# Normalised attention and displacement layer, one core: key/value matmuls moved between the products with V, the second layer spread over the next batch, denominators split over two engines

## The reference

```python
x = x + attention(group_norm(x))        # 32 groups over 24 channels each
x = x + displace(group_norm(x))
# attention, 12 heads of 64 channels: k and v from the last two thirds of W_qkv (q is not used);
#   var_k and var_v = their variances over a head's channels, one number per position
#   scores = var_v @ var_k.T / 8;  softmax;  attn @ v;  @ W_proj.T + b_proj
# displace: 48 bands of 16 channels, each shifted by its own whole offset (zeros come in), then a 3x3 depthwise filter
#   that is a product of a column filter and a row filter
```

## Time and profile before

| | us |
|---|---|
| median of 3 runs | 2329.48 (2328.37 to 2331.11) |
| profiled execution, its own time | 2330.09 |
| its span, first to last instruction | 2328.3 |
| PE busy | 2002.9 (86%) |
| VectorE busy | 1949.5 (84%) |
| ScalarE busy | 1102.4 (47%) |
| POOL busy | 296.2 (13%) |
| mean granted clock of PE, of 2.4 GHz | 0.931 |

### The profile page before, as it was taken

One profiled execution on the slowest core, in us unless ns is written; L12 is line 12 of the kernel. 1 busy time (PEld: TensorE's weight loads), 2 busy tenths in 40 slices (PEclk: granted clock), 3 DMA queues, 4 the chain that ended last, 5 costly groups with the idle time before them and its releaser, 6 DMA issues.

```text
span 2328.3 us, 30324 instructions
## 1 busy us (share of the span) xinstructions
PE 2002.9 (86%) x8804; PEld 788.2 (34%) x8804; DVE 1949.5 (84%) x3547; ACT 1102.4 (47%) x1139; POOL 296.2 (13%) x172
## 2 busy tenths in 40 slices
PE   3998898888988899898997989888898889988850
PEld 2432343323432234322442234332343224432220
DVE  7479959898698986899788996989869898699938
ACT  5249411792237911396115941179223791149601
POOL 2000023000320012100230002300032001210003
PEclk8999999899999999998998999989999999999985
DMA  4222214222242212423044221422224221242104
GB/s 177 113 110 66 90 39 145 92 83 73 61 141 101 65 65 90 166 73 101 3 130 143 63 93 39 145 98 77 73 61 141 101 65 64 90 171 68 47 25 138
DMA packets 106453, 214.37 MB, mean 92 GB/s; under 512 B 53538, under 2 KB 54306, under 8 KB 106274
## 3 DMA queue, kind: packets, MB, share of 16 engines
q1 hardware_dynamic: 93954, 171.44, 23.1%
q10 hardware_dynamic: 12320, 40.77, 5.0%
HBM read 154.08 MB, written 57.74 MB: 91 GB/s over the span
## 4 chain that ended last, share of the span: by engine, by line
issue 61%; DVE 10%; PE 9%; SPq 8%; DMA 4%; POOL 4%; ACT 3%; ACTq 0%; DVEq 0%; POOLq 0%
DVE ox L732 4%; SPq L399 4%; PE ps L1030 4%; PE ps L970 4%; SPq L394 3%; POOL vx L457 3%; ACT ring L582 2%; DVE st L680 1%; DVE h_sp L794 1%; PE ps L1012 1%; DMA shift_rows<-ox 1%; DMA rb_x<-gs_rows_x 1%; DMA ox<-in_L_conv_W_qkv 1%; POOL ox L476 1%; SPq L406 1%
## 5 line engine op out<-in xcount | busy, mean ns | idle before, releaser
L970 PE MATMUL ps<-wkv_hi,h_sp 128*128 128x512 f16 x2304 | 717.2, 390 | 26.6 <-ACT vx L526 19.8
L582 ACT ACTIVATE ring<-a_sb,coef 128x1024 f32<-128x1024 f32 x624 | 660.3, 1134 | 139.0 <-DVE h_sp L794 80.6
L1012 PE MATMUL ps<-ring,vx 128*64 128x512 f32 x2496 | 600.0, 628 | 44.7 <-ACT ring L582 42.0
L794 DVE TENSOR_TENSOR h_sp<-h_sp,ring 128x1024 f32<-128x1024 f32 x464 | 543.2, 1227 | 0.0
L970 PE MATMUL ps<-wkv_lo,h_sp 128*128 128x512 f16 x1152 | 448.9, 390 | 0.0
L1030 PE MATMUL ps<-ox,wp_hi 128*128 128x512 f16 x1152 | 346.7, 382 | 0.0
L970 PEld LDWEIGHTS ps<-wkv_hi,h_sp 128*128 128x128 f16 x2304 | 230.3, 100 | 319.3 <-issue 30.1
L680 DVE BATCH_NORM_STATS2 st<-ps 128x6 f32<-128x64 f32 x1536 | 217.5, 216 | 135.5 <-PE ps L970 130.2
L1012 PEld LDWEIGHTS ps<-ring,vx 128*64 128x64 f32 x2496 | 182.1, 144 | 434.6 <-issue 318.3
L526 ACT ACTIVATE vx<-ps 128x256 f32<-128x256 f32 (+1 forms) x128 | 62.5, 489 | 419.9 <-DVE st L680 419.9
L732 DVE SCALAR_TENSOR_TENSOR ox<-ox,taps 128x992 f32<-128x992 f32 (+1 forms) x160 | 244.4, 1527 | 3.0
(11 more groups left out here) (124 smaller groups left out, 1528.0 us busy)
## 6 DMA issues: line engine op xcount, KB each, us to landing
a_sb<-a_rows SPq DMA_DIRECT2D x64, 512.0 KB, 5.9
ox<-in_x SPq DMA_DIRECT2D x48, 512.0 KB, 6.0
shift_rows<-ox SPq DMA_DIRECT2D x48, 512.0 KB, 3.2
out<-ox SPq DMA_DIRECT2D x48, 512.0 KB, 2.7
vx<-in_x ACTq DMA_DIRECT2D x42, 512.0 KB, 6.1
a_sb<-a_rows ACTq DMA_DIRECT2D x32, 512.0 KB, 6.8
h_sp<-r_rows SPq DMA_DIRECT2D x64, 256.0 KB, 3.9
ox<-shift_rows SPq DMA_DIRECT2D x240, 64.0 KB, 2.0
```

Source lines behind the costliest of these rows:

```text
L582: nc.scalar.activation(ring_t[i % RING], a_sb[:, h % 4, :], ACT.Exp, scale=coef[:, h, m:m + 1]).then_inc(s_exp, 1)
L794: nc.vector.tensor_tensor(acc[p % 2][s], one, ring_t[i % RING], ALU.add).then_inc(s_acc, 1)
L970: last = nc.tensor.matmul(ps[:, kv_bank[u % 4], :], h_sp[:, k, hp, m * P:(m + 1) * P], wkv[wpart][:, k, c * HALF:(c + 1) * HALF], start=(k ...
L1012: last = nc.tensor.matmul(ps[s * HD:(s + 1) * HD, o_bank[p % 3][j], :], v_sb[:, m, (2 * p + s) * HD:(2 * p + s + 1) * HD], ring_t[(i + s) ...
```

## The change

- Key and value columns are now ordered by pair of heads: 24 units again, but a unit is two position tiles of one pair, 2 x 18 matmuls of 256 columns in one bank, and only two banks are used in turn. The first eight units (pairs 0 and 1) stay in stage A. The other sixteen are issued by PE between the products with V: four in each of the pairs 0 to 3, after m = 0, 2, 4, 6. The loop now turns between stages B and C.
- var_v rows, key maxima and coefficients are made per pair: two transposes and one small matmul on PE, some small VectorE instructions, and a write and two broadcasts on SP's queue for each pair. They went once per batch (in two parts) before, and four of the broadcasts were on ACT's queue.
- The ring has eight tiles (four m), not ten.
- Denominators: VectorE adds only the tiles m below MD[p] = 7, 7, 7, 7, 5, 5. The other tiles go straight through the ones matmuls, which now have 32 output partitions and write all into one bank. ScalarE copies the result (d_copy) where VectorE did. The last pair goes the way of the others, through DRAM; its in-place reciprocal is gone.
- The second layer of batch b is spread over the pairs of batch b+1, one channel tile at a time, in one buffer for the shifted tile and one for the taps. Its group norm and its mask are one VectorE instruction (gn) where POOL had two (L469, L476); the mask is now applied before the shift. POOL keeps only the power of -1/2; the first layer's norm goes from POOL to ScalarE. In the last batch six buffers are used.
- x1 tiles are loaded one by one as they come free (x1_reload); the next batch's x is loaded by ACT in pair 4 and its statistics are taken in pair 5, where stage C had them. Two partly done units of the output projection are issued in pair 5.
- In the first batch SP writes the zero pads before the offsets.

The diff, cut to what the text speaks of (removed functions are those printed above; the indentation is cut by eight):

```diff
-RING = 10
-CH = KV // HALF
+PC = 4 * HD
+UQ = MT // 2
+NU = NP * UQ
+RING = 8
+NA_RING = 3
...
-kv_bank = (0, 1, 4, 5)
-pj_bank = (2, 3, 4, 5)
-o_bank = ((2, 3), (0, 1), (6, 7))
-d_bank = (4, 5)
+kv_bank = (0, 1)
+o_bank = (2, 4)
+pj_bank = (0, 1, 2, 3, 7, 6)
+D_BANK = 6
...
+MD = (7, 7, 7, 7, 5, 5)
+ADDS_TO = [0]
+for n in MD:
+    ADDS_TO.append(ADDS_TO[-1] + 2 * (n - 1))
+NADD = ADDS_TO[NP]
+def add_count(p, s, m):
+    return ADDS_TO[p] + 2 * (max(m, 1) - 1) + s + 1
+def acc_of(p, s):
+    return acc[:, (2 * p + s) % NA_RING, :]
+def ring_of(p, s, m):
+    return ring[:, ((p * MT + m) * 2 + s) % RING, :]
+def a_count(b, h):
+    return b * 48 + 16 * (h // 4 + 1)
...
+    def span(b, l1, with_next):
+        later = l1 is not None
+        a_write(b, 0)
+        a_broadcast(b, 0, later)
         for p in range(NP):
+            if p == 0:
+                a_write(b, 1)
+                if later:
+                    g_store(l1, 1)
+                a_broadcast(b, 1, later)
+                if later:
+                    g_windows(l1, 1)
+                    out_store(l1, 0)
+                    g_store(l1, 2)
+                    x1_reload(l1, 0)
+                    g_windows(l1, 2)
+                    out_store(l1, 1)
+                continue
+            d_rows(b, p - 1)
+            r_write(b, p - 1)
+            if p < NP - 1:
+                a_write(b, p + 1)
+            if later:
+                x1_reload(l1, p)
+            r_broadcast(b, p - 1, later)
+            if p < NP - 1:
+                a_broadcast(b, p + 1, later)
+                if later:
+                    if p + 2 < CT:
+                        g_store(l1, p + 2)
+                        g_windows(l1, p + 2)
+                    out_store(l1, p + 1)
+        if with_next:
+            stats_to_groups(sp, "x", b + 1)
+        d_rows(b, NP - 1)
+        r_write(b, NP - 1)
+        if with_next:
+            stats_out(sp, "x", b + 1)
+        r_broadcast(b, NP - 1, later)
+        if with_next:
+            stats_to_channels(sp, "x", b + 1)
...
+    def body(b, with_next):
+        y_chain(b)
+        g_store(b, 0)
+        g_windows(b, 0)
+        span(b + 1, b, with_next)
...
+    def v_evict(b, u):
+        q, g = divmod(u, UQ)
+        act.wait_ge(s_bn, b * NU + u + 1)
+        src = ps[:, kv_bank[u % 2], :].rearrange("p (m c) -> p m c", m=2)
+        nc.scalar.activation(v_sb[:, q, 2 * g:2 * g + 2, :], src[:, :, 0:P], ACT.Copy, scale=V_DOWN).then_inc(s_vev, 1)
+    def exps(b, p, m):
+        for s in (0, 1):
+            h = 2 * p + s
+            i = (p * MT + m) * 2 + s
+            if m == 0:
+                if s == 0:
+                    act.wait_ge(s_coef, b * NP + p + 1)
+                act.wait_ge(s_a[h % 4], a_count(b, h))
+            if i >= RING:
+                pj, mj = divmod((i - RING) // 2, MT)
+                act.wait_ge(s_pv, b * (NT // 2) + (i - RING) // 2 + 1)
+                if mj < MD[pj]:
+                    act.wait_ge(s_acc, b * NADD + add_count(pj, s, mj))
+            nc.scalar.activation(ring_of(p, s, m), a_sb[:, h % 4, :], ACT.Exp,
+                                 scale=coef[:, h, m:m + 1]).then_inc(s_exp, 1)
+    def d_copy(b, p, later):
+        act.wait_ge(s_d, b * NP + p + 1)
+        if later or p:
+            act.wait_ge(s_dt, (b * NP + p) * 64)
+        nc.scalar.activation(d_sb[:, :], ps[:, D_BANK, :], ACT.Copy).then_inc(s_dsb, 1)
...
+    def span(b, l1, with_next, beside=None):
+        later = l1 is not None
         for p in range(NP):
+            nxt = (p + 1) * UQ
             for m in range(MT):
+                if not later and p == 0 and m == 3:
+                    act.wait_ge(s_pads, 2 * CT * 16)
+                exps(b, p, m)
+                if m == 0 and 1 <= p <= 4:
+                    v_evict(b, nxt + 1)
+                if m == 1 and p == 0 and later:
+                    middle_tap(l1, 0)
+                if m == 2 and p <= 4:
+                    v_evict(b, nxt + 2)
+                if m == 3:
+                    if p:
+                        d_copy(b, p - 1, later)
+                    if p <= 4:
+                        v_evict(b, nxt + 3)
+                    if p == 4 and with_next:
+                        load_x(b + 1)
+                if m == 4 and 1 <= p <= 4 and later:
+                    middle_tap(l1, p + 1)
+                if m == 5 and p:
+                    add_bias(b, p - 1)
+                if m == 6 and p <= 3:
+                    v_evict(b, nxt + UQ)
...
+    def kv_stats(b, u):
+        q, g = divmod(u, UQ)
+        dve.wait_ge(s_kv, b * NU + u + 1)
+        for m in (0, 1):
+            for c in range(4):
+                lo = m * 2 * P + c * HD
+                ins = nc.vector.bn_stats(st[:, 2 * g + m, c, :], ps[:, kv_bank[u % 2], lo:lo + HD])
+        ins.then_inc(s_bn, 1)
...
+    def k_max(b, q, later):
+        dve.wait_ge(s_ktp, b * NP + q + 1)
+        if later or q:
+            dve.wait_ge(s_arow, (b * NP + q) * 16)
+        nc.vector.tensor_reduce(kmx1[:, :], ps_kt, AX_X, ALU.max).then_inc(s_kch, 1)
+        nc.vector.tensor_copy(at[:, :], ps_at).then_inc(s_at, 1)
+        dve.wait_ge(s_kch, b * NP + q + 1)
+        nc.vector.tensor_scalar(kdiag[:, :], ident[0:2, 0:2], kmx1[:, 0:1], None, ALU.mult).then_inc(s_kdiag, 1)
...
+    def add_up(b, p, m, later):
+        if not 1 <= m < MD[p]:
+            return
+        for s in (0, 1):
+            i = (p * MT + m) * 2 + s
+            if m == 1:
+                if s and (later or p):
+                    dve.wait_ge(s_d, b * NP + p)
+                one = ring_of(p, s, 0)
+            else:
+                dve.wait_ge(s_acc, b * NADD + add_count(p, s, m - 1))
+                one = acc_of(p, s)
+            dve.wait_ge(s_exp, b * NT + i + 1)
+            nc.vector.tensor_tensor(acc_of(p, s), one, ring_of(p, s, m), ALU.add).then_inc(s_acc, 1)
...
+    def gn(b, t, dst, wait_taps=True):
+        if t == 0:
+            dve.wait_ge(s_msk, b + 1)
+        elif wait_taps:
+            dve.wait_ge(s_pch, b * 4 * CT + 4 * (t - 1) + 2)
+        nc.vector.scalar_tensor_tensor(dst.rearrange("p (y x) -> p y x", x=W),
+                                       x1[:, t, :].rearrange("p (y x) -> p y x", x=W), rb["y"][:, t, 1:2],
+                                       mask_y[:, t:t + 1, :].broadcast_to((P, H, W)),
+                                       ALU.subtract, ALU.mult).then_inc(s_gn, 1)
...
+    def phase_a(b, l1, beside=None):
+        for u in range(2 * UQ - 1):
+            kv_stats(b, u)
+            if l1 is not None:
+                if u == 0:
+                    group_var(dve, "y", l1)
+                if u == 1:
+                    group_spread_y(dve, l1)
+            if u == UQ - 1:
+                variances(b, 0)
+                if l1 is not None:
+                    masks_y(l1)
+                    gn(l1, 0, g_t)
             if beside is not None:
                 beside(u)
...
+    def span(b, l1, with_next, beside=None):
+        later = l1 is not None
         for p in range(NP):
+            nxt = (p + 1) * UQ
+            if p >= 2:
+                o_second(b, p - 2)
+            if p <= 4:
+                kv_stats(b, nxt + 3)
+                variances(b, p + 1)
+            for m in range(MT):
+                add_up(b, p, m, later)
+                if m == 1 and p == 5 and with_next:
+                    x_stats(b + 1, (0, 1))
+                if m == 2:
+                    if p:
+                        d_reciprocal(b, p - 1)
+                    if p <= 4:
+                        k_max(b, p + 1, later)
+                    if p == 0 and later:
+                        taps_y(l1, 0, g_t, t_t)
+                        gn(l1, 1, g_t)
+                        taps_x(l1, 0, t_t)
+                    if p == 5 and with_next:
+                        x_stats(b + 1, (2, 3))
+                if m == 3:
+                    if p <= 3:
+                        kv_stats(b, nxt + UQ)
+                    if p == 5 and with_next:
+                        x_stats(b + 1, (4, 5))
+                        channel_aggregate("x", b + 1)
+                if m == 4:
+                    if p:
+                        o_normalise(b, p - 1)
+                    if p <= 4:
+                        k_scales(b, p + 1)
+                if m == 5:
+                    if p <= 3:
+                        kv_stats(b, nxt + UQ + 1)
+                    if 1 <= p <= 4 and later:
+                        taps_y(l1, p + 1, g_t, t_t)
+                        if p + 2 < CT:
+                            gn(l1, p + 2, g_t)
+                if m == 6:
+                    if p <= 3:
+                        kv_stats(b, nxt + UQ + 2)
+                    if p == 0 and later:
+                        taps_y(l1, 1, g_t, t_t)
+                        gn(l1, 2, g_t)
+                    if p <= 4 and later:
+                        taps_x(l1, p + 1, t_t)
+                if beside is not None:
```

(81 more changed lines are left out.)

858 lines of the change are left out of this document (367 added, 491 removed).

## The result

The changed kernel takes 2366.28 us (median of 4 runs, 2363.57 to 2372.53), the kernel before 2328.93 us beside it. The ratio is 1.0165, with a 95% interval of 1.014 to 1.0189: the change makes the kernel some 1.65% slower. The forecast was 2317 us, with "faster" the likeliest sign.

The account below looks back on a forecast made before the run. PE was taken to bound stages C, A and the middle pairs, VectorE the old stage B and pair 5. 279 + 7 x 274.3 + 113 = 2312 us span, 2313 as run time, plus 4 for handovers: 2317; range takes in 2265 to 2375.

Parts of the forecast that it names:

- four small DMAs 2.3 to issue ... and 1.8 to land: Stage C, chain of pair 5's output: denominator rows through DRAM; whole chain 14.8 us, hidden beside PE's 16.7.
- PE 13.7 + 4 sets 3.4 + 2.4 = 19.5: Pair 4: TensorE's products, four denominator sets and a further 2.4 give 19.5 us.
- The rival that came near: Middle pairs: the reciprocal's DMAs queue behind SyncE's windows; 36 us per pair, cycle +8.5, 2376 us; chance 0.25.
- the rows of landing were measured among such moves: Argument against the slower reciprocal-chain rival: measured landing times already included neighbouring 512 KB moves.
- Pair 5: Last pair of a batch: VectorE bounds it, ending 21 us after pair 4.
- The head: First batch, to its last denominator set: 279 us, before 269.7; SP free for a_write at 83.5.
- Stage A and pair 0: Batch start: first product at 44.5 us into stage A, then pair 0 takes 45 us, held by evictions and VectorE.
- PE idles 12 us: Stage A's end: a_write behind eight windows on SP delays the first product; called the change's largest loss.
- if a_sb lands sooner: Listed way to be wrong: the broadcast tiles land earlier in stage A because VectorE reaches gn(0) sooner.
- The unit prices: TensorE: 256-column matmul 0.11 us, unit of 36 matmuls 3.96, 32-partition denominator set 0.86, mode-change excursion 0.26.
- 0.76 us per excursion: Alternative price of a tiling-mode change on TensorE if a drain lasts 0.38 us: 12 us more per batch.
- Stage C: From the last denominator set: 43.8 us, before 46.9, including PE waiting 2.5 for pair 4's output split.

Follow-up runs that it names:

- e1: Changed kernel with load_x moving 4 columns per tile instead of 1024 (10 KB, not 3 MB per batch), same six DMAs: 2325.1 us.
- e4: Changed kernel with the first batch's six x1 loads issued behind the first row write and broadcasts instead of ahead: 2363.2 us.
- e8: Changed kernel with next-x loads behind pair 3's split, first-batch x1 behind the first row broadcasts, next batch's first rows ahead of the windows: 2283.4 us.
- e5: Changed kernel with the next batch's first a_write and a_broadcast ahead of the eight windows in SyncE's order: 2321.8 us.
- e2: Changed kernel with the next batch's x loads moved from step 3 to step 7 of pair 4, behind pair 3's split: 2339.5 us.
- e12: Changed kernel with the next batch's x loads behind add_bias in step 5 of pair 4: 2366.0 us.
- e7: Changed kernel with the denominator split undone: VectorE adds all eight steps of every pair, TensorE does one ones set per pair: 2515.2 us.
- e3: Changed kernel with VectorE doing k_max of the next pair ahead of the previous pair's reciprocal: 2374.8 us.

## Why the prediction was wrong, and where it was right

**The step that failed** is "four small DMAs 2.3 to issue ... and 1.8 to land", carried into pair 4 as "PE 13.7 + 4 sets 3.4 + 2.4 = 19.5". It gave pair 4 no wait at all. I took the median landing of the earlier trace rows for a small transfer and never asked what else is moving when each is issued. load_x is in the diff, at pair 4, step 3, on ScalarE, in the same place as the d_copy that releases d_rows: 3 MB go out some 2.5 us ahead of four transfers of 2 KB, in all batches but the last. Measured: landing 7.9 us instead of 1.8, and pair 4 30.9 us in the mean of batches 2 to 7 instead of 19.5. Without the bulk (e1) it is 23.9. So 7.0 of the 11.4 us are the bulk, shown; the other 4.4 are a second term that the sum has at nothing, mostly waits of TensorE for VectorE in that pair (1.1 and 2.2 us in e1's fifth batch). In the first batch, where VectorE has no work of layer 1, pair 4 without the bulk takes 19.0 us: there the 19.5 holds. In the whole kernel the seven loads cost 41 of the 49 us between the forecast (2317) and the result.

**The rival that came near** (2376) named the right chain and the wrong pairs and cause. It feared SyncE's windows in front of d_rows in pairs 1 to 3. VectorE's wait on the rows there is:

```profile
708.84 0.25 DVE L844 RECIPROCAL dt_sb<-dt_sb 128x16 f32<-128x16 f32 x1 [6.82 <-DMA dt_sb<-d_sb]
...
774.03 0.25 DVE L844 RECIPROCAL dt_sb<-dt_sb 128x16 f32<-128x16 f32 x1 [1.24 <-DMA dt_sb<-d_sb]
```

6.8 us in pair 1 (I said near 5), then 1.2 in pairs 2 and 3, and the pairs stay TensorE's at 33.7 us. That the result lies 10 us from this rival's 2376 is luck. Its argument against itself, "the rows of landing were measured among such moves", holds for windows of 64 KB and fails for six loads of 512 KB.

**Pair 5** was put down to VectorE at 21 us. It is TensorE's, 23.3 of 23.3 us busy. I had the two partial projections in my account of stage C, as work already done, and did not charge them where they are done: by the starts in TensorE's timeline the two projections take 5.4 us, the eight products 14.3 and the four sets 3.6, together 23.3.

**The head** is 11 us late. SyncE is free at 83.9, as I wrote (83.5), but a_write then meets the six loads of x1 that I mentioned and priced only by their issue. e4 gives 7 of the 11 back in the first batch. The other 4 are the same failed step once more: the first batch loads the second one's x in its pair 4, and e1, without that bulk, ends it at 286.1 instead of 290.6. With both edits (e8) it ends at 278.9, where 279 was predicted.

**Stage A and pair 0** had the right mechanism. "PE idles 12 us" is 8.2, ended by ScalarE behind a_sb. SyncE's queue and TensorE:

```profile
636.69 8.30 SPq L428 DMA_DIRECT2D bt<-shift_rows  x8
645.11 0.33 SPq L384 DMA_DIRECT2D a_rows<-at  x1
646.97 0.84 SPq L393 DMA_DIRECT2D a_sb<-a_rows  x2
```

```profile
653.41 3.47 PE L1182 MATMUL ps<-ring,xv 128*64 128x512 f32 x8 [8.20 <-ACT ring L624]
```

The windows begin 23.7 us into the stage, not 24.2, the broadcasts go out at 34.0 instead of 36, and the first tile lands after 4.0 us instead of 6.3. This is the case "if a_sb lands sooner" of my own list, though hardly for the reason given there: gn(0) comes only 0.5 us sooner, the landing is 2.3 us shorter. e5 shows that the bubble is SyncE's order. These two stages came out 6.4 us better than forecast and hid part of the miss in pair 4.

**The unit prices** held. KV matmuls of 256 columns are 0.11 us apart, sets 0.88 us, and the way out to two transposes and back is 666.84 - 664.65 - 1.71 = 0.48 us with 0.22 of transposes in it: 0.26 us for the changes of mode, as priced. TensorE:

```profile
664.12 0.38 PE L1143 MATMUL ps<-wkv_hi,h_sp 128*128 128x256 f16 x2
664.34 0.27 PE L1143 MATMUL ps<-wkv_lo,h_sp 128*128 128x256 f16 x1
...
664.65 1.94 PE L1182 MATMUL ps<-ring,xv 128*64 128x512 f32 x8
666.52 0.28 PE L1152 MATMUL ps<-ident,av 128*16 128x128 f32 x1
...
666.84 1.51 PE L1182 MATMUL ps<-ring,xv 128*64 128x512 f32 x6
```

```profile
694.20 1.07 PE L1164 MATMUL ps<-ring,ones 128*32 128x512 f32 x8
695.08 1.04 PE L1164 MATMUL ps<-bt,ones 128*32 128x512 f32 x8
```

That refutes the 0.76 us per excursion that I had worked out beside the rule of the Trainium skill, "TensorEngine Tiling (Array Packing)", Key Properties, on the drain: there is a gap, but a third of that size. (Its "12 us more" was a slip as well: the sum had 0.26 already, so it would have been 16 x 0.5 = 8; and the 0.38 us stand in the earlier trace rows.) Four column tiles for 32 columns, as the same page of the Trainium skill has it under Column Tiling, agree with the 0.88 us per set, half of the 1.71 that two at a time would take.

**Stage C** came out right (43.5, said 43.8) with one term wrong. I had TensorE wait 2.5 us for the split of pair 4's output. That split is done when pair 5 ends, and what TensorE loses there is a wait that nothing in the profile releases, at the place where its loop turns:

```profile
852.36 0.39 PE L1197 MATMUL ps<-xv,wp_hi 128*128 128x512 f16 x1 [2.33 <-issue]
```

The wait is 1.8 to 2.3 us at the end of batches 2 to 6 and not there in the other three. That the two have nearly the same length is luck. The middle pairs (33.7, said 33.5) and the tail (111.8, said 113) need no correction, and the loop turn is under the 6.7 us that I allowed. So apart from pair 5 and what VectorE holds up in pair 4, the sum is near wherever no small transfer meets a large one.

## What to carry to other kernels

A small transfer on a critical chain has no fixed landing time. For each one, look at which bulk transfer, on either issuing queue, has been issued ahead of it and is still moving, and price it by a row where two such transfers met. Prefetches are placed by what they run into, not by when their buffer comes free: e2 differs from the kernel after in nothing else and is 27 us faster, and e12, two steps earlier, gains nothing.

When work moves out of one stage, charge it in the stage where it now stands. And sums of busy times tell a bound only if the engines don't wait for each other in turn; in e7 they do.

## What the runs showed that was not expected

Six loads of 512 KB on ScalarE's queue delayed four transfers of 2 KB on SyncE's queue from 2.2 to 7.9 us. The first batch shows it most purely, because there nothing large is moving on SyncE's queue: the rows land in 5.3 to 5.6 us, and in 1.7 to 1.9 without the bulk (e1). A queue of its own is no protection. In the later batches the store of 512 KB that stands ahead of the rows on their own queue is held up as well (8.3 us to land in the third batch, 2.8 in e1), and the rows behind it.

The Trainium skill, "DMA: Bandwidth & Descriptors", section "Queues, rings and completion order", says that both queues run on rings of the same 16 engines, and that a transfer's semaphore increment lands only after every earlier write from that engine, across its queues. That the queues share engines agrees with the trace (7.9 against 2.2 us). The rule on the increment is not what made the rows late here: the trace also has the packets, and the data themselves moved late. In the first batch the 128 packets of 64 bytes that are the rows begin 4.0 us after the first issue, and 1.2 us in e1; in the third batch 6.6 us, and 1.8 in e1. The fourth row lands 0.6 to 0.7 us after its last packet began in the kernel after, 0.3 to 0.4 in e1.

An idle row can name a place that costs nothing: TensorE's 8.1 us in front of the spread, ended by k_max, came back not at all when k_max was moved (e3).
